# A decoder layer on one core: where the retention's scores stand among the projection matmuls

## What is computed

```python
qkv = x @ wqkv.T
q, k, v = jnp.split(qkv, 3, axis=-1)
q, k = _xpos_rotary(q, k, s)
...
scores = jnp.einsum('bhid,bhjd->bhij', q, k) * decay
ret = jnp.einsum('bhij,bhjd->bhid', scores, v)
mean = ret.mean(axis=(2, 3), keepdims=True)
var = ret.var(axis=(2, 3), keepdims=True)
ret = (ret - mean) / jnp.sqrt(var + EPS)
ret = ret * gn_weight[None, :, None, None] + gn_bias[None, :, None, None]
...
g = x @ wg.T
mish = g * jnp.tanh(jax.nn.softplus(g))
return mish * y @ wo.T
```

## Time and profile before

| what | value |
|---|---|
| device time, 3 runs | 1399.16, 1399.88, 1401.53 us; median 1399.88 |
| profiled execution, span of its instructions | 1407.2 us |
| mean granted TensorE clock of the profiled execution | 0.983 |
| PE busy | 1329.2 us (94% of the span) |
| weight loads (PEld) busy | 1070.7 us (76%) |
| DVE busy | 853.9 us (61%) |
| ACT, POOL busy | 486.5 us (35%), 509.8 us (36%) |

### The profile page before, as it was taken

One profiled execution on the slowest core, in us unless ns is written; L12 is line 12 of the kernel. 1 busy time (PEld: TensorE's weight loads), 2 busy tenths in 40 slices (PEclk: granted clock), 3 DMA queues, 4 the chain that ended last, 5 costly groups with the idle time before them and its releaser, 6 DMA issues. The chain is left out here.

```text
span 1407.2 us, 24145 instructions
## 1 busy us (share of the span) xinstructions
PE 1329.2 (94%) x8442; PEld 1070.7 (76%) x8442; DVE 853.9 (61%) x1519; ACT 486.5 (35%) x764; POOL 509.8 (36%) x359
## 2 busy tenths in 40 slices
PE   7999999998899999999889999999999999999974
PEld 5777778776667777776567888888877899999963
DVE  6776666687888888887644665555561442222246
ACT  4222233243466666565754111111111233323310
POOL 1122222234543434432330038411160875563044
PEclk9999999999899999999999999999999999999997
DMA  7992000003664555447100014220001443542247
GB/s 259 325 327 84 0 0 0 0 16 120 182 176 140 168 162 161 148 140 206 28 23 0 24 66 151 97 80 23 23 23 49 182 141 139 185 164 82 73 138 239
DMA packets 85035, 159.83 MB, mean 114 GB/s; under 512 B 8576, under 2 KB 61952, under 8 KB 81536
## 3 DMA queue, kind: packets, MB, share of 16 engines
q1 hardware_dynamic: 78688, 124.19, 28.0%
q0 software_dynamic: 6272, 34.61, 7.0%
HBM read 109.22 MB, written 69.47 MB: 127 GB/s over the span
## 5 line engine op out<-in xcount | busy, mean ns | idle before, releaser
L1526 ACT ACTIVATE b_pf<-b_rt,b_zero 128x1024 f32<-128x1024 f32 x128 | 142.9, 1116 | 119.8 <-PE b_rt L1197 119.3
L1366 DVE TENSOR_REDUCE b_mx<-b_rt 128x4 f32<-128x1024 f32 x128 | 156.3, 1221 | 35.9 <-PE b_rt L1185 35.4
L2058 DVE SCALAR_TENSOR_TENSOR residual<-c_yp,c_shared,residual 128x512 f32<-128x512 f32 x144 | 103.8, 745 | 114.9 <-PE c_yp L43 110.5
L41 PE MATMUL c_fc<-c_xh,c_w 128*128 128x512 f32 x352 | 137.7, 391 | 0.0
L43 PE MATMUL c_fc<-c_xh,c_w 128*128 128x512 f32 x352 | 137.1, 389 | 0.0
L42 PE MATMUL c_fc<-c_xl,c_w 128*128 128x512 f32 x352 | 136.9, 389 | 0.0
L41 PE MATMUL c_fc<-c_ring,c_xTl 128*128 x312 | 105.6, 338 | 3.2 <-issue 3.2
L2196 ACT ACTIVATE c_s<-c_fc 128x512 f32<-128x512 f32 x44 | 26.3, 598 | 232.5 <-PE c_fc L43 226.9
L43 PE MATMUL c_fc<-c_ring,c_xTh 128*128 x312 | 101.3, 325 | 0.0
L42 PE MATMUL c_fc<-c_ring,c_xTh 128*128 x312 | 101.0, 324 | 0.0
L1878 POOL TENSOR_TENSOR c_w<-c_wraw,c_zero 128x1536 fp32r<-128x1536 f32 x9 | 24.8, 2750 | 202.5 <-DMA c_wraw<-in_c_ws 108.5
(11 more groups left out here) (402 smaller groups left out, 3498.5 us busy)
## 6 DMA issues: line engine op xcount, KB each, us to landing
weights_b<-b_pack SPq DMA_DIRECT2D x128, 200.0 KB
c_eraw<-in_c_we POOLq DMA_DIRECT2D x8, 2176.0 KB, 9.5
b_pack<-b_hi SPq DMA_DIRECT2D x56, 256.0 KB, 2.5
c_rows_in<-in_b_ctx SPq DMA_DIRECT2D x39, 256.0 KB, 9.8
c_rows_out<-in_b_ctx SPq DMA_DIRECT2D x39, 256.0 KB, 9.9
c_xe<-c_rows_in SPq DMA_DIRECT2D x39, 256.0 KB, 3.0
c_rows_out<-c_ye SPq DMA_DIRECT2D x39, 256.0 KB, 2.1
c_wraw<-in_c_ws SPq DMA_DIRECT2D x11, 768.0 KB, 4.2
```

What stands on the lines that cost most here:

```text
L41: nc.tensor.matmul(out, ll, rh, start=start, stop=False)
L1366: nc.vector.tensor_reduce(out=mx[:, :, 2 * p:2 * p + 2].rearrange("p t e -> p e t"), in_=rt[:, 0:2, :].rearrange("p e (t s) -> p e t s", s ...
L1526: nc.scalar.activation(pf[:, s:s + 2, :], rt[:, 2:4, :], ACT.Exp, scale=XD ** -0.5, bias=zero[:, :]).then_inc(e_done, 1)
L2058: nc.vector.scalar_tensor_tensor(out=X[:, t, :], in0=yp[:, (n * 4 + k) % 3, :], scalar=shared[:, t:t + 1], in1=X[:, t, :], op0=ALU.mult, o ...
```

## The change

In `body`, for each pair p, the whole projection chunk p of the next batch is issued first, then the scores of the pair p+1, then at once the product with v of the pair p. Before, the chunk was cut in two halves, with the scores between them and the product after them.

```diff
                 for p in range(KT):
                     if p == 0:
                         pe.wait_ge(xl_done, b + 2)
-                    gemm_chunk(b + 1, p, False, (0, 1))
+                    gemm_chunk(b + 1, p, False)
                     if p + 1 < KT:
                         scores(b, p + 1)
-                    gemm_chunk(b + 1, p, False, (2, 3))
                     ret(b, p)
```

## The result

| | before | after |
|---|---|---|
| median of 7 runs each | 1399.88 us | 1404.3 us |
| lowest, highest | 1398.2, 1402.2 | 1403.31, 1408.35 |
| ratio (95% interval) | | 1.0037 (1.0024 to 1.0049) |
| the same change in a second series (below) | | 1.0044 (1.0031 to 1.0058) |
| span of the profiled execution | 1407.2 us | 1401.5 us |

The change makes the kernel slower, by 3.4 to 6.9 us by the first interval; 1407.3 was forecast. The measured 1404.3 lies near the lower end of the forecast's range (1403.5 to 1410) and under the 1405.8 to 1408.8 that its sum alone gives. The two profiled executions order themselves the other way, and that says nothing of the change: from the second pair's scores in the last body to the end it took 1091.4 us in the one of before, and 1078.5 in the one of the change.

What follows compares the result with a forecast made beforehand. It took PE's 38.8 us loop body and a nearly equal PE-DVE ring as the bound. Body 0's 0.59, five loop bodies' 5.65 and body 6's 1.15 gave 7.4 us over 1399.9: 1407.3 us, range 1403.5 to 1410.

Steps and rivals of the forecast that it cites:

- The four waits: In a loop body PE would wait at chunk 4, chunk 5, the group-statistics matmul and the transposes; the last decides, 1.13 us.
- PE's saving: At each of 21 places PE's pair period falls from 4.83 to 4.61 us: 0.22 saved, 4.6 in all if PE alone counted.
- the reverse step: In the last body a product is followed straight by scores after 0.80 us; the direct scores-to-product step was estimated from this.
- rival 1: DVE has room after all at the transposes of x, so PE keeps its 4.6 us: 1395.3 us; chance 0.07.
- the ring: Loop-body chain: PE's third scores start DVE's queue, whose end lets PE transpose x; almost as long as PE's own 38.8 us.
- The delay of the third scores: In each body the third pair's scores come 1.37 - 0.22 = 1.15 us later, moving DVE's queue by the full 1.15.
- the slack at the transposes of x: Between DVE finishing normalized x and PE's load: 0.02 us in a loop body, so each of five bodies costs 1.13 us.
- The wait behind body 6: The output projection already waits 1.65 us for POOL's low half of z, fed by DVE's queue, so the delay adds 1.15.
- More room in DVE (2): DVE's queue is 0.5 us quicker per body relative to PE than profiled: +3.9 us, 1403.8 us; chance 0.15.
- The direct step that saves nothing (3): Going directly from scores to product costs as much as leaving and returning: 8.9 us slower, 1408.8 us; chance 0.08.
- A clock that falls with the new waits (4): PE's new waits lower the granted clock for 3 us in each body: 10 us more, 1418 us; chance 0.03.

Runs made afterwards that it cites:

- first pair only: The reorder at the first pair's place alone, the other two places as in the kernel before: loop body 38.53 us, ratio 0.9987 to the kernel before.
- the DVE move: The changed kernel with DVE's statistics of batch b+2 and reciprocals 2 and 3 issued earlier: loop body 38.12 us, ratio 0.9974 to the kernel before.
- the second profile: The changed kernel run and profiled again with nothing further altered: loop body 39.78 us, stage 283.7 us, ratio 1.0044 to the kernel before.
- the control: The kernel before, PE order untouched, with only DVE's statistics and reciprocals issued earlier: loop body 38.75 us, ratio 0.9997 to the kernel before.
- the best version: The changed kernel plus DVE's earlier statistics and reciprocals, run in two series: ratios 0.9974 and 0.9946 to the kernel before.

## Why the prediction was right, and where its sizes were off

- *The bound.* That a loop with PE busy throughout has a second chain of almost the same length, and that the change lengthens that one: shown. The four waits are in the profile after, at their places, and three experiments move the loop body by lengthening the ring, shortening it, or taking its last wait away.
- *PE's saving.* 0.22 per place forecast, 0.20 to 0.21 measured, taken from the reverse step. The Trainium skill (TensorEngine Tiling (Array Packing), Key Properties) says that a change of tiling mode drains TensorE; the rows agree, with 0.63 us a body for three changes fewer, once nothing else binds. That the saving shows as a gain (rival 1) holds where the ring is not made longer (first pair only: 38.53 us a body) or is given room (the DVE move: 38.12), and not for the change alone. The prediction says that the 0.22 is worth something "twice per body"; its own sum counts it once, at the third scores, and so do the rows below.
- *The delay of the third scores.* 1.15 forecast. Between the starts of the scores in a loop body it is, first to second pair, 9.30 us against 7.93 (+1.37) and, second to third, 4.63 against 4.83 (-0.20). So 1.17. (Third to fourth it is 4.62 against 4.82, behind the point where DVE's queue has taken over.)
- *The term that was mis-sized: the slack at the transposes of x.* I took 0.02 us in a loop body, from the start of PE's load. But that load at 186.85 is prefetched behind running matmuls, and its matmul started 0.10 later; when the load has to wait, its matmul follows at once (190.90 and 190.91). The slack that counts was 0.12, and the loop bodies cost 1.03 to 1.05 instead of 1.13 each. Body 0 has it too: 0.50 in the second profile instead of 0.59. That profile's parts are 0.50 for body 0, 5.21 for the five loop bodies and 1.19 from there to the output projection behind body 6: 6.90 of the stage's 6.95. The forecast had 7.4.
- *The wait behind body 6.* The size came out, the reason given for it did not hold. I took the 1.65 us as the wait that DVE's queue sets. Two rows of the kernel before:

```profile
301.57 1.93 ACT L785 ACTIVATE a_gcn<-a_rt,a_gb,a_ga 128x256 f32<-128x256 f32 x4
...
308.24 0.47 PE L41 MATMUL a_gemm<-weights_a,a_zl 128*128 128x512 f32 x1 [0.34 <-POOL a_zl L929]
```

  And the same two of the changed one:

```profile
308.73 1.93 ACT L784 ACTIVATE a_gcn<-a_rt,a_gb,a_ga 128x256 f32<-128x256 f32 x4 [0.93 <-DVE a_gb L602]
...
315.39 0.47 PE L41 MATMUL a_gemm<-weights_a,a_zl 128*128 128x512 f32 x1 [0.98 <-POOL a_zl L928]
```

  PE waits twice there, once for each half of POOL's low half of z (zl). The second half comes 3.27 or 3.28 us behind the first whatever the kernel (308.24 to 311.51 before, 315.39 to 318.66 after), so the 1.65 says nothing of how late z is; the first wait does, and it went from 0.34 to 0.98. And in the kernel before, ACT starts on z's input (L785) as soon as its copy of k's transposes is done, with no wait for DVE, whose coefficients are ready at 301.53, just ahead of it. That is why the control, whose coefficients are ready 0.8 us earlier, gains nothing there. After the change DVE is late enough to hold ACT for 0.93 us, and z comes 1.12 us later in the first profile and 1.19 in the second. That this meets the forecast's 1.15 rests on ACT having come free just when the coefficients were ready, which I had not looked at: here the term was right by luck.
- *The whole kernel.* Forecast +7.4, measured +4.4 in the first series and a ratio that means +6.2 in the second, against 6.9 in the stage. I had carried the stage's shift over whole. Behind the stage the twelve profiles scatter by more than the difference: nine take 1078.5 to 1084.1 us for it and three 1091.3 to 1091.4, with lower-clock stretches at changing places. So whether some of the shift is really given back stays open.
- *The rivals.* More room in DVE (2) is what remains in part: 0.10 of the 0.5 us that it supposed. The direct step that saves nothing (3) is excluded by 4.63. A clock that falls with the new waits (4): 1.00 in every loop body, though the waits are there. But its counter-argument, that the clock stays at 1.00 behind the 2.15 us of body 0, does not hold for every execution (last section).

## What to carry to other kernels

An engine that is busy throughout is not alone the bound: follow the tightest handover back to it around the loop, and add up that ring as well. When a reorder saves time on the full engine, look at what it makes late, and ask whether that feeds a queue without gaps; if so, first move work out of that queue's gapless stretch into its idle time. And idle time covers a delay only where it lies: 11 us of idle DVE in a body did not help; 2 of them, filled with work from the ring, did.

## What the runs showed that I had not expected

- A weight load can start 0.10 us ahead of its matmul without need, so the slack of a PE instruction is to be read at the matmul and not at its load.
- The kernel with one of the three places changed (the second) has a longer loop body than the kernel with all three. The difference lies ahead of the third scores: from the transposes of x to them it is 17.98 us with the one place and 17.69 with all three, and from them to the next transposes 22.09 and 22.08. Of the 0.29 us, 0.20 lie between the first scores and the third: the first place pays its saving back into the ring. The third place, whose saving comes behind the third scores, pays nothing.
- In four of the twelve profiles body 0 is some 1.5 us longer than its kernel makes it; in these four the mean granted clock of body 0 is 0.96; in the first one of the change a stretch of 3.4 us at 0.51 lies over chunk 0. All twelve have the same wait of 2.15 us just ahead of that place, and in eight of them the clock stays at 1.00. It occurs with and without the faster order (it is in the second profile of the best version, and not in the first), so it belongs to the execution.
